# A conv-scan layer overlapped with an attention layer: values half by half, skip sums spread, a first row spread by TensorE, and a reordered start

## The reference

```python
# layer 0, once forward and once on the flipped tokens, shared weights
u = silu(causal_conv(u)); dt, Bm, Cm = split(u @ x_proj)      # 24 + 16 + 16
delta = softplus(dt @ dt_proj + dt_bias)
h_t = exp(delta * A) * h_{t-1} + (delta * u) * Bm[n]           # 16 states n
y = sum_n h[n] * Cm[n] + u * D                                 # the "skip"
x = x + res_scale * (scale * out_proj(y * silu(z)) + sigmoid(dwconv(xn)) * xn)
# layer 1
p = softmax(causal(q k^T / 8)); x = x + (p @ v) @ Wo; x = x + mlp(ln(x))
```

## Time and profile before

| | |
|---|---|
| Time, median of 3 runs | 4300.12 us (4295.2 to 4302.93) |
| Time of the profiled execution | 4300.21 us |
| Its span | 4298.4 us |
| DVE busy | 3586.2 us, 83% |
| PE busy | 3369.9 us, 78% |
| POOL busy | 2733.2 us, 64% |
| ACT busy | 2549.2 us, 59% |
| Start to first scan of b = 0 | 0 to 110 us |
| Rows of b = 0 | 110 to 464 us |
| Each later sample, first scan to first scan | about 495 us |
| Layer 1 of the last sample alone | about 3960 to 4298 us |

### The profile page before, as it was taken

One profiled execution on the slowest core, in us unless ns is written; L12 is line 12 of the kernel. 1 busy time (PEld: TensorE's weight loads), 2 busy tenths in 40 slices (PEclk: granted clock), 3 DMA queues, 4 the chain that ended last, 5 costly groups with the idle time before them and its releaser, 6 DMA issues.

```text
span 4298.4 us, 40497 instructions
## 1 busy us (share of the span) xinstructions
PE 3369.9 (78%) x11626; PEld 1702.9 (40%) x11626; DVE 3586.2 (83%) x2721; ACT 2549.2 (59%) x3547; POOL 2733.2 (64%) x1692
## 2 busy tenths in 40 slices
PE   5500598878888798888988798887988788876997
PEld 2200245623365234632356233642346233551472
DVE  4999698899889998899889998899888998898121
ACT  4533456756675656757566666757667566665362
POOL 2888476676766766577766767567675767666000
PEclk9755799988999798988999789997999889997998
DMA  3999598787978878787978879787987879788000
GB/s 86 233 244 248 127 223 188 189 202 197 222 165 202 218 183 209 174 204 187 238 170 201 197 194 227 175 196 187 217 196 179 205 191 234 165 201 207 6 7 15
DMA packets 224024, 785.11 MB, mean 183 GB/s; under 512 B 25292, under 2 KB 40958, under 8 KB 223518
## 3 DMA queue, kind: packets, MB, share of 16 engines
q0 software_dynamic: 117504, 427.87, 51.4%
q1 hardware_dynamic: 106270, 354.32, 25.0%
HBM read 339.60 MB, written 39.85 MB: 88 GB/s over the span
## 4 chain that ended last, share of the span: by engine, by line
PE 39%; DVE 23%; issue 12%; DMA 12%; ACT 7%; POOL 6%; DVEq 0%; ACTq 0%; SPq 0%; POOLq 0%
DVE pBC L1181 15%; PE pW L653 10%; DMA y<-hb 9%; PE pW L572 9%; POOL hb L1360 5%; PE pW L460 5%; PE pW L503 4%; ACT pt L980 3%; PE pW L588 2%; PE pW L537 2%; PE pW L710 2%; DMA y<-area 1%; DVE hb L1190 1%; PE pW L716 1%; DVE pBC L1146 1%
## 5 line engine op out<-in xcount | busy, mean ns | idle before, releaser
L1181 DVE TENSOR_TENSOR_SCAN pBC<-pBC,hb 128x1024 f32<-128x1024 f32 x768 | 1757.1, 2288 | 55.2 <-POOL hb L1360 33.7
L1371 POOL DMA_DIRECT2D y<-hb x768 | 729.3, 950 | 820.8 <-DVE hb L1190 732.7
L1360 POOL TENSOR_TENSOR hb<-du_f,b_row 128x1024 f32<-128x1024 f32 x384 | 1014.9, 2645 | 118.4 <-DMA b_row<-bc_rows 72.7
L1360 POOL TENSOR_TENSOR hb<-uc_b,b_row 128x1024 f32<-128x1024 f32 x384 | 994.8, 2591 | 66.7 <-DMA y<-hb 64.6
L1190 DVE TENSOR_TENSOR hb<-pBC,c_row 128x1024 f32<-128x1024 f32 x768 | 940.0, 1224 | 44.4
L799 ACT ACTIVATE pBC<-delta,vec 128x1024 f32<-128x1024 f32 x384 | 429.5, 1119 | 412.6 <-DVE hb L1190 412.5
L799 ACT ACTIVATE pBC<-xres,vec 128x1024 f32<-128x1024 f32 x384 | 429.3, 1120 | 323.5 <-DVE hb L1190 322.8
L653 PE MATMUL pW<-area,pt 128*128 128x64 f32 x3456 | 437.8, 281 | 138.3 <-ACT pt L980 138.3
L653 PEld LDWEIGHTS pW<-area,pt 128*128 128x128 f32 x3456 | 409.1, 194 | 192.4 <-ACT pt L980 184.1
L1225 DVE TENSOR_REDUCE stat<-pW 128x1 f32<-128x640 f32 (+7 forms) x361 | 258.5, 752 | 228.1 <-PE pW L575 228.1
L479 PE MATMUL pW<-area,xn_area 128*128 128x512 f32 x576 | 267.7, 620 | 30.9 <-DVE area L1268 22.6
(11 more groups left out here) (167 smaller groups left out, 4906.9 us busy)
## 6 DMA issues: line engine op xcount, KB each, us to landing
y<-hb POOLq DMA_DIRECT2D x768, 512.0 KB, 7.2
b_row<-bc_rows SPq DMA_DIRECT2D x256, 512.0 KB, 5.9
c_row<-bc_rows SPq DMA_DIRECT2D x256, 512.0 KB, 5.4
du_f<-in_x SPq DMA_DIRECT2D x8, 1536.0 KB, 13.0
kept_residual<-in_x SPq DMA_DIRECT2D x8, 1536.0 KB, 14.3
y<-area POOLq DMA_DIRECT2D x24, 512.0 KB, 7.9
xres<-kept_residual SPq DMA_DIRECT2D x8, 1536.0 KB, 11.9
out_x<-xa SPq DMA_DIRECT2D x8, 1536.0 KB, 7.8
```

Source lines behind the costliest of these rows:

```text
L1181: dve.tensor_tensor_scan(flow(d, buf), flow(d, buf), flow(d, hb[r % NHB][:, :]), 0.0, ALU.mult, ALU.add).then_inc(scan_done, 1)
L1360: pool.tensor_tensor(hb[r % NHB][:, :], du[d][:, k, :], b_row[g % 2][:, :], ALU.mult)\
L1371: pool.dma_start(y[:, k, :], hb[r % NHB][:, :], accum_op=ALU.add).then_inc(y_in[k], 16)
```

## The change

Six edits. (1) Attention values: PE now takes the products of one half of `pt` as soon as that half is copied; in iterations with rows the order of the halves alternates with the group, and so does the bank the values go to (`halves`, `value_bank`). (2) The next sample's items run in rows 66 to 76 for b = 0 too, and the block behind the rows is gone. (3) The skip sums move from rows 21, 22, 23 to rows 24, 27, 30, and the steps of tiles 1 and 2 move one row later. (4) The B row of the first state isn't loaded: PE broadcasts it (`first_row`, products with one row of ones), ACT copies it to `b_row[0]`. The B and C rows are evacuated ahead of the dt rows, and `store_rows` waits for them alone. (5) The first decay and scan come ahead of the third forward softplus; `local` comes ahead of `gated`. (6) In the last iteration the hidden groups alternate between `pW` and the PSUM of the scans (`hidden_bank`), and PE fills the next group ahead of the reduction of the one before.

```diff
-RS = 21
+SKIP = (24, 27, 30)
...
-BEHIND = ([("step_silu", 0, 17), ("step_x", 0, 19)] + [("step_skip", k, RS - KT + k) for k in range(KT)]
-          + [(kind, k, 22 + 3 * k + i) for k in range(KT)
+BEHIND = ([("step_silu", 0, 17), ("step_x", 0, 19)] + [("step_skip", k, 18 + k) for k in range(KT)]
+          + [(kind, k, (22, 26, 29)[k] + i) for k in range(KT)
...
-    return [(kind, n) for kind, n in SLOTS[r] if kind in STEP or layer1 and (more or kind not in NEXT)]
+    return [(kind, n) for kind, n in SLOTS[r] if kind in STEP or (more if kind in NEXT else layer1)]
...
+        def halves(b, g):
+
+            return (0, 1) if alone(b) or g % 2 == 0 else (1, 0)
+
+        def value_bank(b, g):
+
+            return pW[:, 3 if alone(b) else 2 + g % 2, :]
+
+        def hidden_bank(b, g):
+
+            return pB if alone(b) and (g + g // NFG) % 2 else pW
...
-            return 16 * (r // KT + 1 + (r >= RS))
+            return 16 * (r // KT + 1 + (r > SKIP[r % KT] - LAG))
...
-                sp.wait_ge(xd_evac, at(4, b, 2 * d + 2))
+                sp.wait_ge(xd_evac, at(4, b, 4 if d else 1))
...
-                sp.dma_start(b_row[s][:, :], bc_rows[d, n:n + 1, :].broadcast_to([128, L])).then_inc(b_in[s], 16)
+                if g:
+                    sp.dma_start(b_row[s][:, :], bc_rows[d, n:n + 1, :].broadcast_to([128, L])).then_inc(b_in[s], 16)
...
+            def first_row(b):
+
+                pe.wait_ge(xd_evac, at(4, b, 1))
+                pe.wait_ge(uc_ready, at(6, b, 6))
+                for c in range(2):
+                    mm = pe.matmul(pT[:, c * HALF:(c + 1) * HALF], small[0:1, 32:33].broadcast_to([1, 128]),
+                                   bc_raw[0][0:1, c * HALF:(c + 1) * HALF], start=True, stop=True)
+                mm.then_inc(row_ready, 1)
+
...
-                for half in range(2):
+                for n, half in enumerate(halves(b, g)):
                     if g:
-                        pe.wait_ge(pt_ready, at(2 * NG, a, 2 * g - 1 + half))
-                    if g and half and not alone(b):
+                        pe.wait_ge(pt_ready, at(2 * NG, a, 2 * g))
+                    if g and n and not alone(b):
                         pe.wait_ge(ctx_ready, at(NG, a, g))
...
-                        pe.wait_ge(pt_ready, at(2 * NG, a, 2 * g + 2))
                         if alone(b):
                             pe.wait_ge(ctx_ready, at(NG, a, g))
-                        for t, (h, i, c0) in enumerate(GROUPS[g]):
-                            for j in range(i + 1):
-                                mm = pe.matmul(pW[:, 3, DH * t:DH * t + DH], pt[:, c0 + 128 * j:c0 + 128 * j + 128],
-                                               vtok[:, j, DH * h:DH * h + DH], start=(j == 0), stop=(j == i))
+                        for m, half in enumerate(halves(b, g)):
+                            pe.wait_ge(pt_ready, at(2 * NG, a, 2 * g + 1 + m))
+                            part = [(t, h, j, c0 + 128 * j) for t, (h, i, c0) in enumerate(GROUPS[g])
+                                    for j in range(i + 1) if (c0 + 128 * j) // HALF == half]
+                            for q, (t, h, j, col) in enumerate(part):
+                                mm = pe.matmul(value_bank(b, g)[:, DH * t:DH * t + DH], pt[:, col:col + 128],
+                                               vtok[:, j, DH * h:DH * h + DH], start=(m == 0 and q == 0),
+                                               stop=(m == 1 and q == len(part) - 1))
                         mm.then_inc(pv_done, 1)
...
+                        if alone(b):
+                            pe.wait_ge(p_ready, at(NG, a, NG))
+                            pe.wait_ge(pt_ready, at(2 * NG, a, 2 * NG))
+                            if g >= 2:
+                                pe.wait_ge(h_ready, at(2 * NFG, a, g if g == NFG else g - 1))
+                        elif g:
...
+                    if not alone(b):
+                        if q < NFG:
+                            hidden(g)
+                    elif g < 2 * NFG and (q or c == 0):
+                        hidden(g)
...
+                    first_row(b)
...
-                    if more and not layer1:
-                        item("next_mean", 0, b)
-                        in_project(b + 1, 0, 6)
...
+                if d == 0:
+                    act.copy(bc_raw[d], bank[0:32, :]).then_inc(xd_evac, 1)
+                    act.copy(dtr[d][0:RANK, :], bank[32:56, :]).then_inc(xd_evac, 1)
+                    act.wait_ge(row_ready, at(1, b, 1))
+                    act.wait_ge(m1_done, at(ROWS, b, 0))
+                    act.copy(b_row[0][:, :], pT).then_inc(row_copied, 1)
+                else:
+                    act.copy(dtr[d][0:RANK, :], bank[32:56, :]).then_inc(xd_evac, 1)
+                    act.copy(bc_raw[d], bank[0:32, :]).then_inc(xd_evac, 1)
...
-                    if n == 14 and not alone(b):
-                        for k in range(KT):
-                            act.wait_ge(y_in[k], at(YIN, b, 16 * (RS // KT + 1)))
+                    if n >= 14 and n % 2 == 0 and not alone(b):
+                        k = n // 2 - 7
+                        act.wait_ge(y_in[k], at(YIN, b, 16 * ((SKIP[k] - LAG - k) // KT + 2)))
...
                     for k in range(KT):
+                        if k == 2:
+                            decay(b, 0)
                         soft_abs(b, 0, k)
                         soft_exp(b, 0, k)
                         soft_log(b, 0, k)
-                    decay(b, 0)
...
+                    for k in range(KT):
+                        local(b, k)
                     if layer1:
                         gated(b - 1)
-                    for k in range(KT):
-                        local(b, k)
-                    for k in range(KT):
+                    for k in range(2):
                         soft_sum(b, 0, k)
...
+                        if r == 0:
+                            soft_sum(b, 0, 2)
+                            times_u(b, 2)
...
+                if r == 0:
+                    pool.wait_ge(row_copied, at(1, b, 1))
+                elif k == 0 and g % 2 == 0:
+                    pool.wait_ge(b_in[0], at(16 * (NS - 1), b, 16 * (g // 2)))
+                elif k == 0:
+                    pool.wait_ge(b_in[1], at(16 * NS, b, 16 * (g // 2 + 1)))
...
-                pool.wait_ge(y_in[k], at(YIN, b, landed(RS - KT + k)))
+                pool.wait_ge(y_in[k], at(YIN, b, 16 * ((SKIP[k] - LAG - k) // KT + 1)))
```

More of the change, by code:

```diff
@@ L198, in hybrid_block @@
         hid = du_f[:, :, :].rearrange("p k t -> p (k t)").rearrange("p (s f t) -> p s f t", s=2, f=FGRP)
-        pBC = [ctx.enter_context(nc.psum_tensor(f"pBC{i}", [128, L], F32)) for i in range(2)]
+        pB = ctx.enter_context(nc.psum_tensor("pB", [128, 4, HALF], F32))
+        pBC = [pB[:, 2 * i:2 * i + 2, :].rearrange("p b t -> p (b t)") for i in range(2)]
         pW = ctx.enter_context(nc.psum_tensor("pW", [128, 4, HALF], F32))
@@ L526, in out_project @@
                         pe.wait_ge(x2_ready, at(2, b, 0))
+                        if not (isinstance(b, int) and b == NB - 1):
+                            pe.wait_ge(row_copied, at(1, b + 1, 1))
                     if t in (2, 3) and not (isinstance(b, int) and b == NB - 1):
@@ L683, in item, with hidden @@
                     g = c * NFG + q
-                    toks = slice(c * HALF, (c + 1) * HALF)
-                    def hidden():
+                    def hidden(g):
+                        c, q, bank = g // NFG, g % NFG, hidden_bank(b, g)
+                        toks = slice(c * HALF, (c + 1) * HALF)
                         pe.wait_ge(xr_step, at(5, a, 5))
@@ L689, in hidden @@
                             pe.wait_ge(ip_evac, evacs(b))
-                        if g:
+                        if alone(b):
[4 more added lines that the diff above has]
+                        elif g:
                             pe.wait_ge(h_ready, at(2 * NFG, a, g))
-                        if q == 0 and c:
+                        if q == (1 if alone(b) else 0) and c:
                             pe.wait_ge(x2_ready, at(2, a, c))
@@ L891, in scale_ctx @@
                 for t, (h, i, c0) in enumerate(GROUPS[g]):
-                    cx = act.activation(ctxk[:, i, DH * h:DH * h + DH], pW[:, 3, DH * t:DH * t + DH], ACT.Identity,
+                    cx = act.activation(ctxk[:, i, DH * h:DH * h + DH], value_bank(b, g)[:, DH * t:DH * t + DH], ACT.Identity,
                                         scale=stat[:, 2, st + t:st + t + 1])
@@ L975, in item @@
                         g = n - 1
-                        for half in range(2):
-                            act.wait_ge(tr_ready, at(2 * NG, a, 2 * g + half + 1))
+                        for m, half in enumerate(halves(b, g)):
+                            act.wait_ge(tr_ready, at(2 * NG, a, 2 * g + m + 1))
                             if g:
@@ L1013, in item @@
                             act.wait_ge(r_done, at(2 * NFG, a, g - 1))
```

(12 more changed lines are left out.)

18 lines of the change are left out of this document (7 added, 11 removed).

## The result

The changed kernel takes 4230.2 us in the median against 4300.7 for the kernel before beside it, a ratio of 0.9835 (95% interval 0.9818 to 0.9852): faster, by 70 us. The forecast was 4192 us, 108 us faster. Its profiled execution has a span of 4230.7 us, against 4298.4.

The account below looks back on a forecast made before the run. DVE, 83% busy, was taken to bound seven samples with its idle time, PE the end. From 4300.2 us: -84 (values) -24 (norm) +0 (skips, steps) +5 (start) -5 (hidden layer) = 4192 us; range 4148 to 4242.

Parts of the forecast that it names:

- longer skips: Rival: skip landings hold the first scores 9 instead of 3 us a sample, 4234 us; chance 0.12.
- two signs: Wrong in the main if the attention period stays above 5.3 us, or new DVE waits exceed 5 us in rows 27 to 33.
- Values half by half: Attention rows: values start after the first half's copy, saving 0.46 us a row, -84 us; bounds 0 and -131.
- +1.29 + 1.83: Attention row: values start 1.29 us behind the transposes, next scores 1.83 later, at +3.12; period 5.07 us.
- Next norm: Next sample's norm inside the rows of b = 0: 31.8 us go, 8.5 come into the rows; -24 us, bounds -15 and -32.
- Skip sums and softplus steps: Moved skip sums and steps: -3 for POOL and softplus waits, +3 in row 33 per sample; 0 us, bounds -27 and +35.
- the steps keep their distance: Softplus steps of tiles 1 and 2 stay one row apart; tile 2 escapes a 1.0 us query copy.
- The start: Sample starts: first scan 1.4 us earlier at T + 15.6, second later at T + 22.9; +5 us, bounds -10 and +25.
- Last hidden layer: Last hidden layer: PE's waits for GELU and between halves shrink; -5 us, bounds -2 and -9.
- another wait takes the attention row: Rival: ACT's context scaling or the exponential holds the attention row, a fifth of the gain stays, 4259 us; chance 0.12.
- DVE becomes the bound: Rival: DVE bounds the attention row and POOL's waits go too, 4125 us at the floor, 4145 halfway; chance 0.08.
- further block at each start: Eight sample starts: DVE's product blocked once more by POOL, 8 x 2.2 = 18 us, within the start's +25 bound.

Follow-up runs that it names:

- the filler: Changed kernel with PE's products of projections 10 and 11 done twice, output the same: 4228.2 us, ratio 0.9814.
- the run with the old start: Changed kernel with skip sums and steps in their old rows, plus the old state loop start (B's first row by DMA, old order): 4214.2 us, 0.9791.
- both moves back: Changed kernel with skip sums (rows 21, 22, 23) and softplus steps (rows 22, 25, 28) in their old rows: 4208.6 us, ratio 0.9784.

## Why the prediction was right and where it was off

By the spans the kernel got 67.6 us shorter: 66 in the attention rows, 23 by the next norm and 7 at the end, less 25 in rows 21 to 33 and 4 in all the rest. Of the 38 us between 4192 and 4230, 18 are missing in the attention rows and 25 are those of rows 21 to 33; the other terms give some 5 back. That the time lies close to the 4234 of the longer skips is luck, for DVE's first maximum, by whose wait that rival was priced, waits for nothing. And of the two signs by which the prediction called itself wrong in the main, one came: a new wait of over 5 us in rows 27 to 33. The price of skip sums and steps was wrong, though the range held the time.

- **Values half by half: right in kind, mis-sized.** Forecast -84 us, measured -66 in the change and -62 alone. The step that failed is "+1.29 + 1.83": the start at +1.29 came to the digit, the way to the next scores took 1.98 us. I saw ACT's scaling move closer to the transposes by 0.23 us and took the alternating banks as enough cover; it held the copies (1.21 for 1.07 us). Moving the reciprocal gave 10 us of that back. The period is 139.08 / 27 = 5.15 us, where 5.07 was forecast. Pricing the last pass at nothing was right.
- **Next norm: right.** Forecast -24 (its terms, -31.8 and +8.5, give -23.3); the stages give -23, the run without it 21.
- **Skip sums and softplus steps: the step that failed.** Forecast 0, measured +25 before to after, and +20 by putting them back. The waits of "row 27" came as worked out, but so did a second one behind the third skip. The 3 us in row 33 did not come: with the moves or without, DVE's first maximum waits for nothing, and its second waits 1.4 to 2.0 us. And "the steps keep their distance" looked at the order of the queues alone. One row later, with the skip sums spread as well, tile 1's step falls into half clock behind a PE wait of 2.15 us. The POOL waits lay under the wait that this made, which is why the filler, which took 5 us of it away in most samples, shortened these rows by only 5 us in all eight together.
- **The start: right in kind, mis-sized.** T to first scan fell to 14.7 where I had 15.6, because PE's step size did not hold |x| behind the row. The second scan came at T + 21.9, 1 us sooner than forecast, since |x| was 1.1 us sooner. Over seven samples T to second scan went from 22.5 to 21.9 us on average, so with sample 0's 1.3 us more the term is about -3 where I had +5. Yet the line "row 95 to next first scan" fell by only 6.2 us in samples 1 to 6, while the first scans behind it came sooner after T by 3.3 us each, 20 us in all. The 14 us between are ahead of T, where nothing was changed but the order of two items on DVE. They are taken up in the last section.
- **Last hidden layer: right.** Forecast -5, measured -7.3. The waits of 1.63 us are gone, the wait for the add between the halves is 2.46 us, where it was 1.94:

```profile
4200.93 0.61 PE L734 MATMUL pW<-pt,fc_bf 64*128 64x512 bf16 x1 [2.46 <-DVE xa L1296]
```

- **Of the rivals,** "another wait takes the attention row" came in part (18 of 84 us), "longer skips" came in its sum but in rows 21 to 33, not at the first scores. *DVE becomes the bound* did not come (halfway, its terms give 4148, the figure of the range, and not 4145). The further block at each start, 18 us at most, did not come. The product's row (L1130 before; durations in ns, shortest, median, longest) now has nothing above 1.72 us:

```profile
L1170 DVE TENSOR_TENSOR du_f<-delta,area x24: 1224/1225/1724, 103.8 to 3468.8; 128x1024 f32<-128x1024 f32 x24
```

The reading that the second and third product run beside POOL was wrong for the third, which starts when POOL has nothing to do and which POOL waits for. The second meets the last part of POOL's first product (b = 2):

```profile
1014.45 2.35 POOL L1405 TENSOR_TENSOR hb<-du_f,b_row 128x1024 f32<-128x1024 f32 x1 [8.65 <-DVE du_f L1170]
1016.17 1.72 DVE L1170 TENSOR_TENSOR du_f<-delta,area 128x1024 f32<-128x1024 f32 x1
```

POOL's product still has 0.63 us to run when DVE's starts, and DVE's takes 0.5 us longer than its 1.22. All eight starts show this, with 0.32 to 0.64 us to run and 0.18 to 0.50 longer. By the rule of the Trainium skill (SBUF — State Buffer, "Who interferes with whom") two such instructions exclude each other. The trace agrees: DVE's product is longer by about the rest of POOL's. The 3.45 us before was one that began together with a product of POOL of 2.36 us. What decides the price is how much of the other is left.

## What to carry to other kernels

A step moved by one row is not free because its queue neighbours are the same: look what TensorE does just ahead of its new place, and read its granted clock there: six of seven samples had half clock behind a wait of two microseconds, and the seventh had the same wait without it. Before taking one wait away, look what lies under it: here 30 us of softplus waits went and 20 us of others came. Moves made together are to be undone one by one and together, for the longest wait here needed both. After a wait is taken out of a loop, the next one is among the things that moved closer, here a reciprocal of 0.15 us, and moving it was worth 10 us.

## What the runs showed of the hardware

The same work takes another time at another clock. From row 95 to T (with the 4 us ahead), a stretch that the change hardly touches in samples 1 to 6, the windows are, of before, then of after, then of the run with the old start:

```profile
981.17:1019.58 38.41, 34.42 (x72) 13.01 (x72) 36.31 (x28) 26.09 (x28) 22.93 (x12) 0.91 0.61 178
3465.64:3501.63 35.99, 33.46 (x72) 12.67 (x72) 35.36 (x27) 26.24 (x27) 22.45 (x12) 0.95 0.63 185
```
```profile
962.80:1003.19 40.39, 35.84 (x72) 12.98 (x72) 34.58 (x26) 26.29 (x27) 23.43 (x13) 0.87 0.58 170
2918.61:2961.11 42.50, 37.13 (x72) 13.43 (x72) 35.37 (x27) 26.11 (x27) 24.92 (x15) 0.84 0.56 163
```
```profile
954.30:994.63 40.33, 35.90 (x72) 13.12 (x72) 34.72 (x27) 26.30 (x27) 22.68 (x12) 0.87 0.57 168
```

The same 72 matmuls take 36.0 us at a granted clock of 0.95, 38.4 at 0.91, 40.4 at 0.87 and 42.5 at 0.84. Summed over the six samples it is 229.5 us before, 243.0 after, 233.3 with both moves back and 241.6 with the old start, though its instructions are the same in all, the order of `gated` and `local` on DVE apart: up to 13 us of a kernel's time, as large as most terms of my sum. The clock is not all of it. PE's busy time in these windows sums to 208.1 us before and 216.6 after, 8.5 of the 13.5 us, and the rest is PE's idle time; and windows at 0.87 and 0.88 take from 39.3 to 42.0 us. What decides which samples get the slow form I can't say from these runs; it is open.
